# Moving the last four groups' queries into the second layer's first chunk, with 1/norm on VectorE

## The reference

```python
h = jnp.maximum(_layernorm(x, axis=-1), 0.0)
x = x + elu(softmax(where(adj > 0, leaky_relu(wh1 + wh2.T), NEG)) @ wh)      # layer 0
h = jnp.maximum(_layernorm(x, axis=-1), 0.0)
Qn = cos_normalize(h @ Wq.T)          # row / max(|row|, 1e-4)
Kn = cos_normalize(h @ Wk.T)
att = softmax(where(adj > 0, Kn @ Qn.T, NEG), axis=1)
x = x + 0.5 * (att @ h) + 0.5 * h                                            # layer 1
```

## Time and profile before

| | us |
|---|---|
| median of three runs | 2189.89 (2189.19 to 2190.89) |
| the profiled execution | 2189.39 |
| its span, first to last instruction | 2187.6 |
| PE busy in the span | 2142.1 |
| DVE busy | 1963.5 |
| ACT busy | 1752.8 |

### The profile page before, as it was taken

How to read it: one execution, slowest core, us unless ns; L and a number is a source line. 1 busy time by engine, 2 the same in 40 slices (tenths; PEclk the granted TensorE clock), 3 DMA queues, 4 the chain that set the end, 5 groups by cost and what they waited for, 6 DMA issues and landing times.

```text
span 2187.6 us, 63203 instructions
## 1 busy us (share of the span) xinstructions
PE 2142.1 (98%) x26185; PEld 1733.5 (79%) x26185; DVE 1963.5 (90%) x1686; ACT 1752.8 (80%) x1928; POOL 33.0 (2%) x43
## 2 busy tenths in 40 slices
PE   5999999999999979999999999999999999999998
PEld 5999999999999956777777777777777777777776
DVE  7999999999999858889888898898898898898987
ACT  6687778878788668888888888888888888888886
POOL 1000000000000030000000000000000000000000
PEclk9999999999999989999999999999999999999999
DMA  6899999999999916565565665665665666656653
GB/s 248 328 382 401 390 405 397 401 402 399 403 400 388 361 40 217 193 223 204 207 215 196 224 212 196 220 220 193 214 221 200 212 204 216 215 194 218 218 193 115
DMA packets 153732, 573.52 MB, mean 262 GB/s; under 512 B 9936, under 2 KB 10576, under 8 KB 153168
## 3 DMA queue, kind: packets, MB, share of 16 engines
q1 hardware_dynamic: 142176, 546.02, 68.3%
q10 hardware_dynamic: 11376, 24.91, 3.0%
HBM read 558.24 MB, written 12.65 MB: 261 GB/s over the span
## 4 chain that ended last, share of the span: by engine, by line
PE 95%; DVE 2%; ACT 1%; issue 1%; DMA 0%; POOL 0%; ACTq 0%; POOLq 0%; DVEq 0%
PE bank L1197 32%; PE bank L1245 30%; PE bank L1266 21%; PE bank L1261 10%; DVE hl_buf L726 1%; PE bank L1152 1%; PE bank L1172 0%; DVE hl_buf L714 0%; DMA ring<-adj 0%; ACT hl_buf L558 0%; ACT ring L619 0%; POOL hl_buf L401 0%; PE bank L1094 0%; PE bank L1134 0%; DMA q_buf<-x 0%
## 5 line engine op out<-in xcount | busy, mean ns | idle before, releaser
L619 ACT ACTIVATE ring<-bank,th_col 128x512 f32<-128x512 f32 x1024 | 647.1, 683 | 231.0 <-PE bank L1245 223.3
L988 DVE SCALAR_TENSOR_TENSOR ring<-ring 128x2048 f32<-128x2048 int32 x256 | 586.4, 2291 | 154.5 <-ACT ring L619 154.5
L1197 PE MATMUL bank<-v_buf,ring 128*128 128x129 f16 (+1 forms) x12288 | 711.9, 220 | 6.3 <-DVE ring L902 6.1
L1197 PEld LDWEIGHTS bank<-v_buf,ring 128*128 128x128 f16 x12288 | 707.8, 98 | 9.8 <-issue 8.9
L1245 PE MATMUL bank<-v_buf,q_buf 128*128 128x512 f16 x3072 | 706.4, 380 | 5.2 <-ACT ring L619 5.2
L1266 PE MATMUL bank<-u_buf,hl_buf 128*128 (+1 forms) x8192 | 704.3, 220 | 0.0
L1266 PEld LDWEIGHTS bank<-u_buf,hl_buf 128*128 128x128 f16 x8192 | 631.8, 98 | 55.9
L902 DVE SCALAR_TENSOR_TENSOR ring<-r_ring,th_word,ring 128x1024 f32<-128x1024 f32 x512 | 619.3, 1277 | 19.3 <-ACT ring L448 19.1
L993 DVE TENSOR_TENSOR hl_buf<-ring,hl_buf 128x2048 f16<-128x2048 f32 x256 | 584.5, 2284 | 0.0
L1261 PE MATMUL bank<-u_buf,hl_buf 128*128 (+1 forms) x2048 | 557.9, 272 | 0.5 <-DVE hl_buf L993 0.5
L448 ACT ACTIVATE ring<-ring 128x2048 f32<-128x2048 int32 x256 | 481.2, 1908 | 88.4 <-DMA ring<-adj 85.0
(11 more groups left out here) (138 smaller groups left out, 433.0 us busy)
## 6 DMA issues: line engine op xcount, KB each, us to landing
ring<-adj SPq DMA_DIRECT2D x512, 1024.0 KB, 5.6
r_ring<-a_rows SPq DMA_DIRECT2D x8, 512.0 KB, 7.0
x_dram<-q_buf ACTq DMA_DIRECT2D x8, 512.0 KB, 7.2
h_dram<-hl_buf ACTq DMA_DIRECT2D x8, 512.0 KB, 7.4
r_ring<-x_dram ACTq DMA_DIRECT2D x16, 256.0 KB, 4.2
r_ring<-h_dram ACTq DMA_DIRECT2D x16, 256.0 KB, 4.4
out<-r_ring ACTq DMA_DIRECT2D x16, 256.0 KB, 4.8
r_ring<-k_rows ACTq DMA_DIRECT2D x15, 256.0 KB, 4.1
```

Of the source, the lines that this page charges most:

```text
L619: ins = nc.scalar.activation(p_ring[:, k, (2 * hf + m) * IW:(2 * hf + m + 1) * IW], bank[:, 2 * hf + m, :], ACT.Exp, scale=q_scale[:, j:j ...
L988: V.scalar_tensor_tensor(p_ring[:, k, :], adj_ring[:, k, :], 0.0, p_ring[:, k, :], ALU.is_gt, ALU.mult).then_inc(s_m, 1)
L1197: ins = mm(acc0(par, it), weights0(k, ps)[:, it // 4, jj, f], v2[:, bass.ds((2 * j + us) * VW, D + 1)], start=False, stop=False, skip_grou ...
```

## The change

- PE's `qk(12)` to `qk(15)`, `t2(14)` and `t2(15)` go into chunk 0 of layer 1, behind its units 0, 2, 3, 5 and 6; `keys(1)` goes from behind unit 3 to behind unit 8, `transpose_factors(2)` from there to behind unit 10. The queries of the four late groups use banks 6 and 7.
- The squares of the four late groups go to one buffer, `r_ring[:, 0, :]`, and not to a ring of two; they are not halved by POOL, so that DVE's `norm_sums` of them reads 128x1024 instead of 128x512. `square(12)` to `square(15)` hang on ACT behind units 1, 3, 6 and 7; from `square(13)` each waits for the `norm_sums` of the group before. DVE does `norm_sums(12)` behind unit 2, `norm_sums(13)` and `copy_ht(14)`, `copy_ht(15)` behind unit 4, `norm_sums(14)` behind unit 7 and `norm_sums(15)` behind unit 8.
- 1/norm is made on DVE alone, without ACT's root: a first guess by integer arithmetic and three Newton steps, 15 instructions, nearly each waiting for the one before. `factors(0)` stays ahead of `denominators()`, `factors(1)` goes behind unit 0 of layer 1 and `factors(2)` behind unit 9.
- All 16 `copy_ht` are DVE's, with one semaphore. `copy_ht(0)` stood on ACT behind its last unit of layer 0; it now stands on DVE behind DVE's last unit of layer 0.
- ACT's table loads stay three; the last goes from the end of the seam to just behind `normalised()`, which is no longer cut in two. `residual(0)` (two loads of 256 KB) goes from the start of layer 1 to behind unit 13 or so of chunk 0.

```diff
-            return 0 if g < EARLY else 2 * ((g - EARLY) % 2)
+            return 0 if g < EARLY else 2 * ((g - EARLY) % 2) if g < LATE else 6
+        def squares(g):
+            return sq_ring[:, g % 2, :] if g < LATE else r_ring[:, 0, :]
...
 ACT
-            def copy_ht(g):
-                act.wait_ge(s_ht, g + 1)
-                nc.scalar.activation(both(g), ht_bank(g).rearrange("p (s n) -> p s n", s=2), ACT.Copy).then_inc(s_hc[0], 1)
             def square(g):
                 act.wait_ge(s_qk, g + 1)
-                if g >= 2:
+                if g > LATE:
+                    act.wait_ge(s_red, g)
+                elif 2 <= g < LATE:
                     act.wait_ge(s_hs, g - 1)
...
-            def roots(b):
...
-            copy_ht(0)
-            square(0)
-            copy_ht(2)
-            for g in range(1, EARLY):
+            for g in range(EARLY):
                 square(g)
-            roots(0)
-            copy_ht(4)
             nc.scalar.activation(warm[:, :], ident[:, 0:1], ACT.Exp)
             quotient()
             square(4)
             exponential()
             nc.scalar.activation(warm[:, :], ident[:, 0:1], ACT.Sqrt)
-            copy_ht(6)
             square(5)
-            copy_ht(8)
             square(6)
+            ln_root()
             square(7)
-            ln_root()
-            copy_ht(10)
+            normalised()
+            nc.scalar.activation(warm[:, :], ident[:, 0:1], ACT.Exp)
             square(8)
...
             key_high(0)
-            square(10)
-            square(11)
-            roots(1)
-            act.wait_ge(s_x1w, 16 * NC0)
-            copy_ht(12)
-            copy_ht(14)
-            for g in range(12, NI):
+            for g in range(9, LATE):
                 square(g)
-            roots(2)
...
-                    parts = {(0, 0): lambda: load_factors(1), (1, 2): lambda: key_high(1), (2, 1): lambda: load_factors(2)}
+                    parts = {(0, 1): lambda: square(12), (0, 2): lambda: load_factors(1), (0, 3): lambda: square(13),
+                             (1, 2): lambda: square(14), (1, 3): lambda: square(15), (2, 3): lambda: key_high(1),
+                             (3, 1): lambda: load_factors(2), (3, 2): lambda: residual(0)}
...
 DVE
+            copy_ht(0)
             copy_ht(1)
             norm_sums(0)
+            copy_ht(2)
             norm_sums(1)
             copy_ht(3)
             norm_sums(2)
+            copy_ht(4)
             norm_sums(3)
             copy_ht(5)
             factors(0)
             denominators()
             copy_rows(0)
             negative()
+            copy_ht(6)
+            residual()
             copy_ht(7)
-            residual()
             norm_sums(4)
+            moments()
+            copy_ht(8)
             norm_sums(5)
-            moments()
+            scales()
             copy_ht(9)
             norm_sums(6)
-            scales()
+            copy_ht(10)
+            key_scaled(0)
             norm_sums(7)
-            copy_ht(11)
-            key_scaled(0)
-            norm_sums(8)
             split()
             key_low(0)
+            copy_ht(11)
+            norm_sums(8)
+            copy_ht(12)
+            norm_sums(9)
+            copy_ht(13)
+            for g in range(10, LATE):
                 norm_sums(g)
...
             def factors(b):
-                dve.wait_ge(s_nr, b + 1)
...
-                V.reciprocal(k_scale[:, cols], norms[:, 1, cols])
-                V.reciprocal(q_scale[:, cols], norms[:, 0, cols]).then_inc(s_nf, 1)
...
+                V.tensor_scalar(x, x, w_scale[:, 0:1], None, ALU.max).then_inc(s_nf, 1)
+                dve.wait_ge(s_nf, done + 1)
+                V.tensor_scalar(t.bitcast(I32), x.bitcast(I32), 1, None, ALU.logical_shift_right).then_inc(s_nf, 1)
+                dve.wait_ge(s_nf, done + 2)
+                V.tensor_scalar(y.bitcast(I32), t.bitcast(I32), -1, ROOT_GUESS, ALU.mult, ALU.add).then_inc(s_nf, 1)
+                V.tensor_scalar(x, x, -0.5, None, ALU.mult).then_inc(s_nf, 1)
+                for turn in range(3):
+                    dve.wait_ge(s_nf, done + 3 * turn + 4)
+                    V.tensor_tensor(t, y, y, ALU.mult).then_inc(s_nf, 1)
+                    dve.wait_ge(s_nf, done + 3 * turn + 5)
+                    V.tensor_tensor(t, t, x, ALU.mult).then_inc(s_nf, 1)
+                    dve.wait_ge(s_nf, done + 3 * turn + 6)
...
-                    parts = {(1, 0): lambda: copy_rows(1), (1, 1): lambda: key_scaled(1), (1, 3): lambda: key_low(1)}
+                    parts = {(0, 0): lambda: factors(1), (0, 2): lambda: norm_sums(12), (1, 0): copies,
+                             (1, 3): lambda: norm_sums(14), (2, 0): lambda: norm_sums(15), (2, 1): lambda: factors(2),
+                             (2, 2): lambda: key_scaled(1), (3, 0): last_keys}
...
 PE
                 if g >= 2:
-                    pe.wait_ge(s_hc[g % 2], g // 2)
+                    pe.wait_ge(s_hc, g - 1)
+                if g >= LATE + 2:
+                    pe.wait_ge(s_sq, LATE + 2)
...
-                pe.wait_ge(s_hc[g % 2], g // 2 + 1)
+                pe.wait_ge(s_hc, g + 1 if g < LATE else (g | 1) + 1)
...
+                late = {0: ((qk, 12),), 2: ((qk, 13),), 3: ((t2, 14), (t2, 15)), 5: ((qk, 14),), 6: ((qk, 15),),
+                        8: ((keys, 1),), 10: ((transpose_factors, 2),)} if first else {}
```

More of the change, by code:

```diff
@@ L277, in graph_layers @@
         SN0 = NC0 * G0
+        ROOT_READY = {FOLDS[b] // 4: ROOT_STEPS * b + 13 for b in range(len(FOLDS) - 1)}
         @block.sync
@@ L395, in _ @@
                                            bass.bass_isa.ReduceOp.max).then_inc(s_wtop, 1)
-            for g in range(NI):
+            for g in range(LATE):
                 pool.wait_ge(s_sq, g + 1)
@@ L912, in copy_ht @@
             def copy_ht(g):
+                if g == LATE:
+                    dve.wait_ge(s_x1w, 16 * NC0)
                 dve.wait_ge(s_ht, g + 1)
-                V.tensor_copy(both(g), ht_bank(g).rearrange("p (s n) -> p s n", s=2)).then_inc(s_hc[1], 1)
+                V.tensor_copy(both(g), ht_bank(g).rearrange("p (s n) -> p s n", s=2)).then_inc(s_hc, 1)
             def norm_sums(g):
-                dve.wait_ge(s_hs, g + 1)
+                if g < LATE:
+                    dve.wait_ge(s_hs, g + 1)
+                    src = half_ring[:, g % 2, :]
+                else:
+                    dve.wait_ge(s_sq, g + 1)
+                    src = squares(g)
@@ L1049, in chunk1, with copies, last_keys @@
                 else:
-                    parts = {(1, 0): lambda: copy_rows(1), (1, 1): lambda: key_scaled(1), (1, 3): lambda: key_low(1)}
+                    def copies():
+                        norm_sums(13)
+                        copy_ht(14)
+                        copy_ht(15)
+                    def last_keys():
+                        key_low(1)
+                        copy_rows(1)
+                    parts = {(0, 0): lambda: factors(1), (0, 2): lambda: norm_sums(12), (1, 0): copies,
+                             (1, 3): lambda: norm_sums(14), (2, 0): lambda: norm_sums(15), (2, 1): lambda: factors(2),
+                             (2, 2): lambda: key_scaled(1), (3, 0): last_keys}
                 for g in range(G1):
@@ L1225, in _ @@
             transpose_factors(0)
-            for g in range(5, NI - 2):
+            for g in range(5, LATE):
                 qk(g)
@@ L1275, in chunk1, with unit @@
                 pe.wait_ge(s_lo, i + 1)
[L1276 to L1281, removed]
+                late = {0: ((qk, 12),), 2: ((qk, 13),), 3: ((t2, 14), (t2, 15)), 5: ((qk, 14),), 6: ((qk, 15),),
+                        8: ((keys, 1),), 10: ((transpose_factors, 2),)} if first else {}
+                def unit(q):
+                    scores(i, q // RING, q % RING, first and q == 0)
+                    if q == LAG and 1 <= i <= NI - 2:
+                        pe.wait_ge(s_ks, i + 2)
+                    if q >= LAG:
+                        values(i, q - LAG, (q - LAG) % RING, par, head=(q == LAG))
                     elif not first:
-                        values(i - 1, RING * G1 - LAG + k, RING - LAG + k, 1 - par, tail=(k == LAG - 1))
+                        values(i - 1, RING * G1 - LAG + q, RING - LAG + q, 1 - par, tail=(q == LAG - 1))
+                    if q in late:
+                        for step, which in late[q]:
+                            step(which)
                 if first:
[L1285 to L1289, removed]
-                        values(i, RING * h + k + RING - LAG, (k - LAG) % RING, par)
+                    for q in range(RING * G1):
+                        unit(q)
+                else:
+                    for q in range(RING):
+                        unit(q)
+                    with pe.Fori(0, G1 - 1) as h:
+                        for k in range(RING):
+                            scores(i, h + 1, k, False)
```

(1 more changed line is left out.)

65 lines of the change are left out of this document (32 added, 33 removed).

## The result

The changed kernel takes 2196.84 us in the median of 9 runs (2194.91 to 2203.05), the kernel before 2190.68 in 9 runs beside it: 6.2 us more. The ratio is 1.0030 with a 95% interval of 1.0021 to 1.0038, so it is slower by more than 0.2%. The forecast was slower, by 10 us; 2196.8 lies in its range of 2192 to 2206.

A forecast was written before the change was run, and what follows sets the result against it. PE, 98% busy, was taken as the bound, so time is won only where it stands still or is slowed; 6.3 - 10.9 + 14.8 = +10.2 us gave 2200 us, range about 2192 to 2206.

The forecast's parts named there:

- Part A: End of layer 0: `qk(0)` waits for DVE's `copy_ht(0)`, 4.7 us later plus 1.6 of half clock, +6.3 us.
- the sum: All stretches added, waits and half clocks included: 6.3 - 10.9 + 14.8 = +10.2 us, about 2200 us; chance 0.60.
- Part B: From `qk(4)` to the first scores: 24.9 us instead of 35.8, -10.9 us, of which 6.1 is only moved work.
- The port: Seam, DVE beside POOL: residual given 0.3 us, nbias nothing; if nbias waited for the half sum, total 11.4, not 10.2.
- Part C: From the first scores to layer 1's second chunk: moved work returns and PE meets new waits, +14.8 us.
- The two big waits: First chunk of layer 1: 3.9 us ahead of `t2(14)`, 4.0 ahead of `transpose_factors(2)`, each with 1.75 of half clock.
- the small ones: First chunk of layer 1: waits of 1.4 at `qk(13)`, 0.4 at `qk(14)`, 1.5 at `qk(15)`, 0.6 at unit 9's scores.
- the Newton chain: DVE's 1/norm: 15 instructions, 14 in sequence, 3.4 us, or 4.0 for `factors(1)`; bounds 2.9 and 4.4.
- The reduction of 128x1024: DVE's `norm_sums` of late groups in the first chunk: nearest row 1.21 us, bounds 0.7 and 1.4.
- all four forecast falls to half clock: PE slows behind the waits at `qk(0)`, `qk(10)`, `t2(14)` and `transpose_factors(2)`: 1.6, 1.4, 1.75 and 1.75 us.
- rival 1: PE's clock stays full behind the new waits: only +4.2 us, 2194; chance 0.18 for all or in part.
- Rival 2: Layer 1's first chunk takes the moved work without waits: 15.4 us less, 2184.7; chance 0.12 for all or in part.

The follow-up runs named there:

- the last kernel: The reordered one with ACT's last table load behind `square(9)`, and `square(12)` and its reduction one unit later: 2179.04 us, ratio 0.9948.
- the reordered one: The changed kernel with the first copy on ACT, both transposes one unit later, and late work placed where its input is ready: 2181.84 us, ratio 0.9959.

## Why the prediction was right, and where its sizes were off

- **Part A** (+6.3; measured +5.6 in the profile, 5.6 to 7.4 us in the medians and spans of the runs that put the copy on DVE by itself, and 3 to 4 us in the two that undid it). The mechanism is shown: the wait came at the foreseen place, 4.37 us, released by DVE's copy, and DVE was through 0.5 us sooner. The half clock behind it cost 1.5 us (`qk(0)` to `qk(1)` 757.49 to 763.64, 6.15 us instead of 4.69), where I had 1.6. That this fits is luck. The fall came only within the twelve matmuls here (1.94 us, not the 2.74 of the sum), and it lasted into the 48 of the unit, for which the sum had nothing; in the other four profiles with DVE's copy the twelve took 2.74, and the fall cost 2.4 to 2.7 us. Nor did the prediction have that the adjacency loads make both ends of this wait vary: it was 4.37 to 6.56 us long in the five profiles with DVE's copy.
- **Part B** (-10.9; measured -11.2). Each wait was met to 0.4 us: 1.49, 1.45, 1.79 and 2.76 us ahead of `qk(5)`, `qk(7)`, `qk(8)` and `qk(10)`, the last with the half clock. The table load ahead of `square(8)` is shown to make 1.8 us of this stretch, the half clock included. The port: nbias and a half sum of POOL both started at 792.97, and neither waited for long (0.17 and 1.31 us), so the 10.2 and not the 11.4 was the sum to take. `key_low(0)`, which started 0.5 us after a half sum, took 1.34 us instead of 0.68, and the first residual step 1.46 instead of 1.21; a copy out of PSUM beside a half sum, at 793.06, kept its 0.68. Both slowed instructions have two inputs in SBUF. By the rule of the Trainium skill that I weighed ("SBUF — State Buffer", Who interferes with whom) whoever starts first holds the other up for its whole instruction. The rows agree to 0.14 us: each ended that much sooner than if it had begun only behind the half sum.
- **Part C** (+14.8; measured +13.8). The two big waits were 3.41 (forecast 3.9) and 3.50 (forecast 4.0), each with the half clock, and the small ones 1.33, 0.22, 1.46 and 0.34, together 10.3 where I had 11.9. The term that was too large is the Newton chain: 3.1 us and 3.5 us (810.80 to 814.29) where I had 3.4 and 4.0; most of its steps on 32 elements take 0.19 and not 0.23. The sum counts a wait from where PE's next start would have been, and the profile from the end of the last matmul, which is some 0.16 us later (twelve score matmuls fill 2.75 us, and the work behind them starts after 2.59). Counted as in the sum the six waits are 11.2 us, and the two slow stretches cost 3.2 where I had 3.5: that is the 1.0 us by which the stretch is under the forecast. The reduction of 128x1024 took the 1.21 us of its neighbour row. That it is the order and not DVE's load that costs is shown: DVE was 80.6 us busy in the 98.4, and in the last kernel's order it is 80.2 us busy in 86.0.
- **The sum** was 10.2, the profiles differ by 8.2, the medians by 6.2. The first 2.0 us are the terms above. The other 2.0 are the choice of executions: the profile before was 1.3 us under its median, the one after 0.7 over. That all four forecast falls to half clock came in this profile is partly luck, for a fall, which I took as fixed by the length of a wait, is not. The two profiles of the kernel with ACT's first copy have the same waits in the first chunk; the stretch took 98.3 us in one (801.99 to 900.30) and 95.3 in the other (799.91 to 895.17), where full clock followed. So rival 1, the full clock, is not one outcome for all executions but can happen at each wait by itself. That this makes the spread of the times (8 us in the 9 after, 0.9 in the 5 of the last kernel, whose longest wait behind `qk(0)` is 1.79) fits, but is not shown.
- **Rival 2**, the first chunk without waits, needed another order of the parts; in that order one wait was left, of 2.40 and then 1.48 us.

## What to carry to other kernels

When work moves from one engine to another, look at the place it gets in the new engine's queue: one copy of 0.7 us behind the last weights of another engine cost 5.6 to 7.4 us where it was put in by itself, as much as the whole change lost, and 3 to 4 where it was undone. PE, 98% busy, paid in full for each instruction that asked too soon, even when every helper had time left; put a consumer one unit behind the place where its input is ready by the timeline, not at the place where the input is asked for. In the first chunk's profiles, costs found one at a time in such a walk added up when repaired together.

## What the hardware showed that was not expected

The same wait is followed by half clock in one profile and by full clock in another. PE's scores behind the wait for `square(13)`, in the two profiles of the kernel with ACT's first copy:

```profile
822.96 1.05 PE L1165 MATMUL bank<-ident,u_buf 128*128 128x128 f16 x16 [3.40 <-ACT r_ring L563]
823.85 4.44 PE L1281 MATMUL bank<-v_buf,q_buf 128*128 128x512 f16 x12
...
820.89 1.05 PE L1165 MATMUL bank<-ident,u_buf 128*128 128x128 f16 x16 [3.41 <-ACT r_ring L563]
821.78 2.75 PE L1281 MATMUL bank<-v_buf,q_buf 128*128 128x512 f16 x12
```

And behind 2.40 us, in the kernel with the later table load and DVE's first copy, where the reordered one without them has 4.33 us:

```profile
817.66 2.76 PE L1274 MATMUL bank<-v_buf,q_buf 128*128 128x512 f16 x12 [2.40 <-ACT ring L602]
```

The granted clock confirms it, here 0.50, the level of 1.2 GHz, in the changed kernel behind its 3.41 us (busy time of PE, clock, DMA share, GB/s):

```profile
827.00:828.00 1.00, 1.00 (x4) 0.50 0.36 33
```

PE's waits of these twelve profiles, from `qk(0)` to the second chunk, by what followed:

| wait, us | times | half clock | full clock |
|---|---|---|---|
| up to 1.85 | all others | 0 | all |
| 2.28 | 2 | 1 | 1 |
| 2.40 | 3 | 2 | 1 |
| 2.75 to 2.76 | 7 | 6 | 1 |
| 3.40 to 3.42 | 4 | 3 | 1 |
| 3.50 | 4 | 3 | 1 |
| 3.68 to 6.56 | 9 | 9 | 0 |

A fall cost 1.4 to 2.8 us. Between 2.28 and 3.50 us a wait's length alone doesn't decide it; what does was not found.
